# Silu ahead of quantising, two hidden rows by turns, and GpSimd's two norms in the other order

## The chip, the cores and the metric

The kernel runs on one NeuronCore of one Trainium2 chip. The time is device microseconds (us) of that core, the median of three runs. Five engines work side by side, each through its own list of instructions in order, and wait for each other by semaphores: TensorE (PE in the profile: matmuls and transposes; PEld is its weight load), VectorE (DVE), ScalarE (ACT), GpSimd (POOL), and SyncE (SP), which here only starts DMAs. TensorE's clock has two levels, 2.4 and 1.2 GHz; a granted clock of 1.00 in the profile is the upper one, 0.50 the lower.

## The reference

The input x has 4 x 1024 rows of 256 values. Three layers follow each other, each on a layer norm of x and each added to x. What matters here is the second half:

```python
x = x + attn(layernorm(x))                      # gated linear recurrence along the sequence
out = softmax(q k^T) v @ Wout                   # cross attention, 16 heads, 64 + 1 null keys
x = x + (out - mu) * rsqrt(var + 1e-6) * ln_scale + ln_bias
z = act_quant(layernorm(x))                     # round(z * 127 / max|z|), row by row
h = silu(z @ w_gate.T) * (z @ w_up.T)           # 1024 hidden values per row
x = x + act_quant(h) @ w_down.T                 # again scaled by 127 / max|h| of its row
```

The weights of the last layer are ternary (-1, 0, 1 times one scale), so its matmuls run on small integers in bf16 and the scales are put on behind them.

## The kernel before

The 4096 rows are 32 tiles of 128 rows (T = 32), a tile's rows on the 128 partitions. Stage 1 (the recurrence) takes four tiles at a time, then weights are folded, and from about 163 us on `stages2_3(n, u4)` runs for n = -2 to 38, on each engine with its own body. This is a software pipeline written out by hand: one step n works on several tiles at once, each one stage further on. The order of the calls in each body is the order in which that engine works; nothing is reordered.

What step n does, with the lines of the profile:

- PE: scores of tile n+2 (L1140), transposes of the attention weights of tile n in two halves (L1360, L1368) and of the null column (L1372), gate and up matmuls of tile n-5 (`gate_up`, L1140 with wgT and wuT), the output matmuls of tile n (L1382, L1387, and L1390, which ends them and signals `out_psum`). In even steps four more transposes follow for the scores of tiles n+4 and n+5 (L1273). Last is the down matmul of tile n-7 (L1140 with wdT). The first half of the scores of a later tile shares PSUM banks with gate, the second half with up, so gate waits until VectorE has read the first half of tile n+2's scores, and up until it has read the second.
- DVE: maximum and subtraction of tile n+2's scores, each in two halves (L991, L994, twice), the small part of the null column (L1057), in odd steps L965, the sum of exponentials of tile n+1 (L1003) and its reciprocal (L1008, `rden`), the statistics for the fourth norm of tile n-2 (L1072, L1080, `mv4`), silu times up of tile n-5 (`hidden_layer`, L1021), the maximum of z of tile n-3 (L1086), the statistics of the attention output of tile n (L1093, L1099, `mv3`), the maximum of the hidden row (L1028), scales (L1108 to L1032) and the last residual of tile n-7 (L1039).
- ACT: the attention output's norm of tile n-1 (`norm_out`, L686), copies of the transposed weights (L742, L745, L747), quantising the hidden row of tile n-6 (L759), silu of the gate of tile n-5 (`silu_gate`, L698, ahead of it a table load L693), the fourth norm of tile n-3 (`norm3`, L706), in even steps L663 and L678, and the exponential of tile n+2 (L773 with its own table load).
- POOL: scale, bias and residual of the attention output of tile n-1 (L516, L518, L520), attention weights times `rden` of tile n+1 (L528, L531), the cast of tile n-6's quantised row to bf16 (L540), then two groups of three tiny instructions that turn a mean and a variance into scale and bias: for the fourth norm of tile n-2 (L548, L550, L554, `sc4`) and for the attention output's norm of tile n (L561, L563, L567, `sc3`). Last is the rounding of z of tile n-3 (L574, L579).
- SP: DMA transposes of the quantised rows, z (L460) and hidden (L454), and the stores (L463).

The hidden layer has one row buffer `sg3` for silu's result and one, `h`, for the product; `hidden(n)` names the latter (for the last five tiles it goes by turns with the space of the exponentials). So silu of a tile waits until VectorE has read `sg3` for the tile before, and VectorE's product waits until ScalarE has quantised the row before. `late(n)` is true from n = 32 on; there ScalarE does silu ahead of quantising already.

Of the kernel before, what the change touches and what calls it, by code (L numbers as in the profile page):

```python
# [23 lines left out]
ALU = mybir.AluOpType  # L24
ACT = mybir.ActivationFunctionType
AX = mybir.AxisListType
# [7 lines left out]
def decoder_layer(nc, x, ctx_in, w_qkva, gamma, Wq, Wkv, null_kv, Wout, ln_scale, ln_bias,  # L34
# [6 lines left out]
    FI = w_gate.shape[0]  # L41
    T = B * N // P
# [17 lines left out]
    with ExitStack() as stack:  # L60
# [11 lines left out]
        def banks(b, n):  # L72
            return psum[:, b:b + n, :]
# [15 lines left out]
        expo = sbuf("expo", [P, 2 * GT])  # L89
# [27 lines left out]
        mv3 = sbuf("mv3", [P, 2, 2])  # L117
        sc3 = sbuf("sc3", [P, 2, 3])
# [4 lines left out]
        amax = sbuf("amax", [P, 2, 2])  # L123
        qs = sbuf("qs", [P, 2, 2])
        qr = sbuf("qr", [P, 2, 2])
        zw = sbuf("zw", [P, 4, 2])
# [23 lines left out]
        def carve(region, spec):  # L150
            views, at = {}, 0
            for name, n in spec:
# [11 lines left out]
        c = carve(region_c, [("sg", FI), ("h", FI), ("n", 2 * D // 2),  # L164
                             ("nvsel", HC * NP), ("nq", FI // 2), ("nhT", FI // 2)])
        nvsel = c["nvsel"]
        sg3 = c["sg"]
        n3 = c["n"].bitcast(BF16).rearrange("p (r d) -> p r d", r=2)

        f = carve(region_b, [("wq", KD * INNER), ("wout", HC * D), ("ctx", 2 * CTX),  # L170
# [37 lines left out]
        z3 = s["z"].rearrange("p (r d) -> p r d", r=2)  # L208
        nT3 = s["nT"].bitcast(BF16).rearrange("p (r k n) -> p r k n", r=2, k=KD)
        nh3 = s["nh"].bitcast(BF16)  # L210
        h3 = [c["h"], s["e"][:, 0:FI]]
        nhT3 = [r["nhT"].bitcast(BF16).rearrange("p (k n) -> p k n", k=FC) for r in (s, c)]
        nq3 = c["nq"].bitcast(I16)

# [3 lines left out]
        consts_set = sem("consts_set")  # L218
# [74 lines left out]
        p_ready = sem("p_ready")  # L293
# [46 lines left out]
        def positive(value):  # L340

            return not isinstance(value, int) or value > 0

        def registers(eng, *values):

            return [value if isinstance(value, int) else eng.to_reg(value) for value in values]
# [12 lines left out]
        def exists(n, count):  # L361

            return not isinstance(n, int) or 0 <= n < count
# [9 lines left out]
        def late(n):  # L373

            return isinstance(n, int) and n >= T

        def hidden(n):

            return h3[1 if isinstance(n, int) and n >= T - 5 and (n - (T - 5)) % 2 == 0 else 0]

        def half(n):
            return n >> 1

# [86 lines left out]
        def _(pool):  # L470
# [40 lines left out]
            def stages2_3(n, u4):  # L511
# [23 lines left out]
                if exists(n - 6, T):  # L535

                    pool.wait_ge(hq_done, n - 5)
                    if positive(n - 6):
                        pool.wait_ge(nhT_ready[v], 16 * ((n - 7) // 2 + 1))
                    pool.tensor_copy(nh3, nq3).then_inc(nh_ready, 1)  # L540
                if exists(n - 2, T):

                    count, free = registers(pool, n - 1, n - 3)
                    pool.wait_ge(consts_set, 2)
                    pool.wait_ge(mv4_done, count)
                    if positive(free):
                        pool.wait_ge(z_ready, free)
                    pool.tensor_scalar(sc4[:, u, 0:1], mv4[:, u, 1:2], 1e-5, None, ALU.add).then_inc(ve4_done, 1)  # L548
                    pool.wait_ge(ve4_done, n - 1)
                    pool.tensor_tensor(sc4[:, u, 1:2], sc4[:, u, 0:1], expo[:, 0:1], ALU.pow).then_inc(rstd4_done, 1)  # L550
                    count, = registers(pool, n - 1)
                    pool.wait_ge(consts_set, 2)
                    pool.wait_ge(rstd4_done, count)
                    pool.tensor_scalar(sc4[:, u, 2:3], mv4[:, u, 0:1], sc4[:, u, 1:2], -1.0, ALU.mult, ALU.mult) \  # L554
                        .then_inc(nmr4_done, 1)
                if exists(n, T):

                    count, = registers(pool, n + 1)
                    pool.wait_ge(consts_set, 2)
                    pool.wait_ge(mv3_done, count)  # L560
                    pool.tensor_scalar(sc3[:, u, 0:1], mv3[:, u, 1:2], 1e-6, None, ALU.add).then_inc(ve3_done, 1)  # L561
                    pool.wait_ge(ve3_done, n + 1)
                    pool.tensor_tensor(sc3[:, u, 1:2], sc3[:, u, 0:1], expo[:, 0:1], ALU.pow).then_inc(rstd3_done, 1)  # L563
                    count, = registers(pool, n + 1)
                    pool.wait_ge(consts_set, 2)
                    pool.wait_ge(rstd3_done, count)
                    pool.tensor_scalar(sc3[:, u, 2:3], mv3[:, u, 0:1], sc3[:, u, 1:2], -1.0, ALU.mult, ALU.mult) \  # L567
                        .then_inc(nmr3_done, 1)
                if exists(n - 3, T):

                    count, = registers(pool, n - 2)
# [14 lines left out]
        def _(act):  # L586
# [103 lines left out]
            def silu_gate(n, v):  # L690

                if n < T - 1:
                    act.preload_act_table(ACT.Silu)  # L693
                act.wait_ge(gate_psum, n - 4)
                act.wait_ge(zw_done, n - 4)
                if positive(n - 5):
                    act.wait_ge(h_ready, n - 5)
                act.activation(sg3, banks(0, 2).rearrange("p b n -> p (b n)"), ACT.Silu,  # L698
                               scale=zw[:, (n - 5) % 4, 0:1]).then_inc(silu_ready, 1)

            def norm3(n, v):
# [28 lines left out]
            def stages2_3(n, u4):  # L730
# [6 lines left out]
                if exists(n, T):  # L737

                    act.wait_ge(pT0_psum, n + 1)
                    if positive(n):  # L740
# [5 lines left out]
                    act.wait_ge(pT1_psum, n + 1)  # L746
                    act.activation(pT[:, HC // 2:HC, :], bank(5).rearrange("p (c n) -> p c n", n=P), ACT.Copy) \  # L747
                        .then_inc(pT1_ready, 1)
                if late(n) and exists(n - 5, T):
                    silu_gate(n, v)  # L750
                if exists(n - 6, T):

                    if n - 1 < T:
                        act.wait_ge(qr_done, n - 3)
                    else:
                        act.wait_ge(qrh_done, n - T)
                    if positive(n - 6):
                        act.wait_ge(nh_ready, n - 6)
                    act.activation(nq3, hidden(n - 6), ACT.Copy, scale=qr[:, u, 0:1]).then_inc(hq_done, 1)  # L759
                if not late(n) and exists(n - 5, T):  # L760
                    silu_gate(n, v)
                if not late(n) and exists(n - 3, T):
                    norm3(n, v)
                if even:
# [14 lines left out]
        def _(dve):  # L779
# [231 lines left out]
            def hidden_layer(n, v):  # L1011

                dve.wait_ge(up_psum, n - 4)
                dve.wait_ge(zw_done, n - 4)
                dve.wait_ge(silu_ready, n - 4)
                if late(n):
                    dve.wait_ge(hq_done, n - 6)
                    dve.wait_ge(p_ready, 2 * T)
                elif positive(n - 5):
                    dve.wait_ge(hq_done, n - 5)  # L1020
                dve.scalar_tensor_tensor(out=hidden(n - 5), in0=banks(2, 2).rearrange("p b n -> p (b n)"),  # L1021
                                         scalar=zw[:, (n - 5) % 4, 1:2], in1=sg3, op0=ALU.mult, op1=ALU.mult) \
                    .then_inc(h_ready, 1)

            def hidden_max(n, v):

                dve.wait_ge(h_ready, n - 4)
                dve.tensor_reduce(amax[:, v, 0:1], hidden(n - 5), AX.X, ALU.max, apply_absolute_value=True) \  # L1028
                    .then_inc(hmax_done, 1)

            def hidden_weight(n, v):
# [397 lines left out]
```

## Time and profile before

| what | value |
|---|---|
| median of 3 runs (lowest, highest) | 540.6 us (540.0, 541.85) |
| time of the profiled execution | 540.44 us |
| its span, first to last instruction | 538.7 us |
| mean granted TensorE clock | 0.983 |
| busy PE, DVE, ACT, POOL | 481.4, 423.9, 324.0, 304.4 us |
| HBM traffic | 36 GB/s over the span |

The span has four stretches: up to about 90 us loads and the first layer, then the first layer and the folding of weights, from about 229 us the full pipeline of all stages in steps of some 10.7 us, and from about 477 us the end, where no scores are left. A timeline row gives start, length, engine, line, operation and in brackets for how long the engine sat idle before it and what ended that; without brackets there was no idle time worth naming. A busy share is an average over such stretches: TensorE is busy for 89% of the span, but its matmul ends are modelled, so a short wait is better read from the starts of its rows.

### The profile page before, as it was taken

What the parts mean: (1) busy time and instruction counts of PE and PEld (TensorE: products, weight loads), DVE (VectorE), ACT (ScalarE), POOL (GpSimd) and SP (SyncE); (2) the same over time, 40 slices, a digit from 0 to 9 for tenths busy, and PEclk for the clock granted to TensorE, in tenths of its full rate; (3) what the DMA queues carried; (4) which work ended last, traced back from release to release, by engine and by line L of the source; (5) the groups of instructions that cost most, each with busy time, mean ns of one, the idle gap of its engine ahead of it and who ended that gap; (6) DMA issues with size and microseconds to landing.
All of it is one profiled execution on the core that took longest, in us unless ns stands there. A gap on an engine that the chain in (4) does not pass through costs nothing.

```text
span 538.7 us, 9271 instructions
## 1 busy us (share of the span) xinstructions
PE 481.4 (89%) x2926; PEld 389.4 (72%) x2954; DVE 423.9 (79%) x936; ACT 324.0 (60%) x450; POOL 304.4 (57%) x482
## 2 busy tenths in 40 slices
PE   1889999989988989999999999999999999988662
PEld 0666787767767878788887887888878778866321
DVE  4899998968337676988888888888888888875673
ACT  4422233245333353797788888877878888685451
POOL 2211223710001668778778787887787878787631
PEclk9999999999999999999999999999999999998895
DMA  8995000240000000012321222121213211212242
GB/s 263 321 337 213 1 0 1 40 78 1 2 0 1 1 2 5 12 24 50 42 49 35 44 48 49 35 50 41 49 35 46 48 46 36 54 40 63 51 97 68
DMA packets 68173, 32.06 MB, mean 60 GB/s; under 512 B 50720, under 2 KB 66336, under 8 KB 68128
## 3 DMA queue, kind: packets, MB, share of 16 engines
q1 hardware_dynamic: 68128, 31.50, 23.3%
q8 instruction: 23, 0.38, 0.3%
q14 instruction: 22, 0.18, 0.1%
HBM read 15.24 MB, written 4.19 MB: 36 GB/s over the span
## 4 chain that ended last, share of the span: by engine, by line
POOL 31%; issue 23%; PE 21%; DVE 17%; DMA 4%; ACT 2%; POOLq 1%; DVEq 1%; SPq 0%; ACTq 0%
PE psum L1140 9%; POOL region_d L540 5%; POOL region_d L518 3%; POOL xs L520 3%; POOL region_d L516 3%; PE psum L1156 3%; POOL sc L563 3%; POOL sc L550 3%; DVE region_a L877 3%; PE psum L1382 2%; POOL region_d L574 2%; PE psum L1387 2%; POOL region_d L531 2%; POOL region_c L579 2%; DMA region_d<-region_d 2%
## 5 line engine op out<-in xcount | busy, mean ns | idle before, releaser
L528 POOL TENSOR_TENSOR region_d<-region_d,rden 128x1024 f32<-128x1024 f32 x32 | 60.9, 1902 | 100.7 <-DVE rden L1008 100.7
L1140 PE MATMUL psum<-Mhi,xT2hi 128*128 128x260 f32 x256 | 75.0, 293 | 0.2
L1140 PE MATMUL psum<-Mlo,xT2hi 128*128 128x260 f32 x256 | 72.4, 283 | 0.0
L1140 PE MATMUL psum<-Mhi,xT2lo 128*128 128x260 f32 x256 | 72.3, 282 | 0.0
L1382 PE MATMUL psum<-VW,region_d 128*128 128x256 f32 x256 | 62.6, 389 | 4.6 <-DVE pTn L1057 4.6
L1387 PE MATMUL psum<-VW,region_d 128*128 128x256 f32 x256 | 60.7, 380 | 0.0
L1021 DVE SCALAR_TENSOR_TENSOR region_c<-psum,zw,region_c 128x1024 f32<-128x1024 f32 x29 | 37.2, 1283 | 28.7 <-ACT region_c L698 28.7
L1382 PEld LDWEIGHTS psum<-VW,region_d 128*128 128x128 f32 x256 | 49.0, 193 | 14.9 <-DVE pTn L1057 6.0
L1387 PEld LDWEIGHTS psum<-VW,region_d 128*128 128x128 f32 x256 | 49.0, 191 | 6.8
L686 ACT ACTIVATE region_d<-psum,sc 128x256 f32<-128x256 f32 x32 | 18.0, 564 | 55.7 <-POOL sc L567 54.8
L991 DVE TENSOR_REDUCE mx<-psum 128x8 f32<-128x520 f32 x64 | 44.2, 691 | 6.4 <-PE psum L1140 5.2
L1140 PEld LDWEIGHTS psum<-Mhi,xT2hi 128*128 128x128 f32 x256 | 48.2, 188 | 1.3 <-issue 1.0
L1140 PEld LDWEIGHTS psum<-Mlo,xT2hi 128*128 128x128 f32 x256 | 48.3, 189 | 0.0
L1140 PEld LDWEIGHTS psum<-Mhi,xT2lo 128*128 128x128 f32 x256 | 48.2, 188 | 0.0
L994 DVE TENSOR_TENSOR region_d<-psum,mx 128x520 f32<-128x520 f32 x64 | 44.8, 700 | 2.2
L494 POOL TENSOR_TENSOR pw_out<-pw_in,expo 128x8 f32<-128x8 f32 x8 | 13.1, 1641 | 52.6 <-DVE pw_in L811 52.6
L540 POOL CAST region_d<-region_c 128x1024 bf16<-128x1024 int16 x32 | 33.2, 1037 | 14.5 <-ACT region_c L759 14.5
L1003 DVE TENSOR_REDUCE den<-region_d 128x16 f32<-128x1040 f32 x32 | 39.4, 1231 | 0.5
L1140 PE MATMUL psum<-wuT,region_d 128*128 128x512 bf16 x128 | 33.9, 388 | 5.8 <-DVE region_d L994 3.2
L698 ACT ACTIVATE region_c<-psum,zw 128x1024 f32<-128x1024 f32 x32 | 35.6, 1112 | 5.2 <-DVE region_c L1021 2.9
L773 ACT ACTIVATE region_d<-region_d 128x1040 f32<-128x1040 f32 x32 | 34.3, 1073 | 7.2 <-DVE region_d L994 6.9
L598 ACT ACTIVATE region_a<-psum 128x1024 f32<-128x1024 f32 x8 | 8.2, 1028 | 47.3 <-PE psum L1156 47.3
(143 smaller groups left out, 1242.2 us busy)
## 6 DMA issues: line engine op xcount, KB each, us to landing
out_dram<-xs SPq DMA_DIRECT2D x32, 128.0 KB, 1.9
xs<-in_x_dram SPq DMA_DIRECT2D x1, 2560.0 KB, 13.9
VW<-in_L_xattn_Wkv_dram SPq DMA_DIRECT2D x1, 2048.0 KB, 11.9
region_b<-in_L_xattn_Wkv_dram SPq DMA_DIRECT2D x1, 2048.0 KB, 17.6
xs<-in_x_dram SPq DMA_DIRECT2D x3, 512.0 KB, 7.0
region_w<-in_L_ffn_w_gate_dram SPq DMA_DIRECT2D x2, 512.0 KB, 10.3
region_w<-in_L_ffn_w_up_dram SPq DMA_DIRECT2D x2, 512.0 KB, 7.9
region_w<-in_L_ffn_w_down_dram SPq DMA_DIRECT2D x8, 128.0 KB, 4.5
```

What stands on the lines that cost most here:

```text
L528: pool.tensor_tensor(p2[:, v, 0:H * MK].rearrange("p (h j) -> p h j", j=MK), e[:, :, 0:MK], rden[:, v, :].unsqueeze(2).broadcast_to([P, H, ...
L540: pool.tensor_copy(nh3, nq3).then_inc(nh_ready, 1)
L686: act.activation(y2[:, v, :], bank(7, D), ACT.Identity, bias=sc3[:, v, 2:3], scale=sc3[:, v, 1:2]).then_inc(y2_ready, 1)
L698: act.activation(sg3, banks(0, 2).rearrange("p b n -> p (b n)"), ACT.Silu, scale=zw[:, (n - 5) % 4, 0:1]).then_inc(silu_ready, 1)
L773: act.activation(e2[:, u, :], e2[:, u, :], ACT.Exp).then_inc(exp_done, 1)
L991: dve.tensor_reduce(mx[:, hh, :].rearrange("p (b h) -> p b h", h=HB), scores, AX.X, ALU.max) \
L994: dve.tensor_tensor(e2[:, u, hh * 2 * HB * J:(hh + 1) * 2 * HB * J].rearrange("p (b h j) -> p b h j", b=2, j=J), scores, mx[:, hh, :].rear ...
L1003: dve.tensor_reduce(den[:, :], e2[:, slot, :].rearrange("p (h j) -> p h j", j=J), AX.X, ALU.add) \
L1021: dve.scalar_tensor_tensor(out=hidden(n - 5), in0=banks(2, 2).rearrange("p b n -> p (b n)"), scalar=zw[:, (n - 5) % 4, 1:2], in1=sg3, op0= ...
L1140: mm = pe.matmul(dst, lhsT, rhs, start=i == 0, stop=i == len(terms) - 1)
L1382: pe.matmul(bank(7, D), pT[:, pair, :], VW[:, batch(n), pair, :], start=pair == 0, stop=False)
L1387: pe.matmul(bank(7, D), pT[:, pair, :], VW[:, batch(n), pair, :], start=False, stop=False)
```

## The change

ScalarE now does silu of tile n-5 first and quantises the hidden row of tile n-6 after it, in all steps. For this two row buffers are used by turns, `hid3[0]` and `hid3[1]` (the former `sg` and `h`), one for each parity of the tile: silu writes its row into one, VectorE multiplies in place in the same one, and the next step quantises from it. `hidden()` and its use of the exponentials' space are gone. Silu now waits for `hq_done` of the tile two before instead of `h_ready` of the tile before, the product has no wait for `hq_done` any more, and quantising names `h_ready`. On GpSimd the group for the output's norm (`sc3`) now stands ahead of the one for the fourth norm (`sc4`).

```diff
-        sg3 = c["sg"]
+        hid3 = [c["sg"], c["h"]]
...
+                if exists(n, T):
+
+                    count, = registers(pool, n + 1)
+                    pool.wait_ge(consts_set, 2)
+                    pool.wait_ge(mv3_done, count)
+                    pool.tensor_scalar(sc3[:, u, 0:1], mv3[:, u, 1:2], 1e-6, None, ALU.add).then_inc(ve3_done, 1)
...
                 if exists(n - 2, T):
 
                     count, free = registers(pool, n - 1, n - 3)
...
-                if exists(n, T):
-
-                    count, = registers(pool, n + 1)
-                    pool.wait_ge(consts_set, 2)
-                    pool.wait_ge(mv3_done, count)
...
-                if positive(n - 5):
-                    act.wait_ge(h_ready, n - 5)
-                act.activation(sg3, banks(0, 2).rearrange("p b n -> p (b n)"), ACT.Silu,
+                if positive(n - 6):
+                    act.wait_ge(hq_done, n - 6)
+                act.activation(hid3[v], banks(0, 2).rearrange("p b n -> p (b n)"), ACT.Silu,
...
-                if late(n) and exists(n - 5, T):
+                if exists(n - 5, T):
                     silu_gate(n, v)
...
-                    act.activation(nq3, hidden(n - 6), ACT.Copy, scale=qr[:, u, 0:1]).then_inc(hq_done, 1)
-                if not late(n) and exists(n - 5, T):
-                    silu_gate(n, v)
+                    act.wait_ge(h_ready, n - 5)
+                    act.activation(nq3, hid3[u], ACT.Copy, scale=qr[:, u, 0:1]).then_inc(hq_done, 1)
...
-                if late(n):
-                    dve.wait_ge(hq_done, n - 6)
-                    dve.wait_ge(p_ready, 2 * T)
-                elif positive(n - 5):
-                    dve.wait_ge(hq_done, n - 5)
-                dve.scalar_tensor_tensor(out=hidden(n - 5), in0=banks(2, 2).rearrange("p b n -> p (b n)"),
-                                         scalar=zw[:, (n - 5) % 4, 1:2], in1=sg3, op0=ALU.mult, op1=ALU.mult) \
+                dve.scalar_tensor_tensor(out=hid3[v], in0=banks(2, 2).rearrange("p b n -> p (b n)"),
+                                         scalar=zw[:, (n - 5) % 4, 1:2], in1=hid3[v], op0=ALU.mult, op1=ALU.mult) \
```

ScalarE, a full step of the pipeline, before (region_c holds the hidden rows, psum ahead of L698 is the gate):

```order
L747 ACTIVATE region_d<-psum 128x512
L759 ACTIVATE region_c<-region_c,qr 128x1024
L693 ACT_TABLE_LOAD
L698 ACTIVATE region_c<-psum,zw 128x1024
L706 ACTIVATE region_d<-xs,sc4 128x256
```

and after:

```order
L742 ACTIVATE region_d<-psum 128x512
L688 ACT_TABLE_LOAD
L693 ACTIVATE region_c<-psum,zw 128x1024
L755 ACTIVATE region_c<-region_c,qr 128x1024
L701 ACTIVATE region_d<-xs,sc4 128x256
```

The table load and silu (L698, now L693) have moved ahead of quantising (L759, now L755); the norm behind them keeps its place.

GpSimd, a full step of the pipeline, before:

```order
L540 CAST region_d<-region_c 128x1024
L548 TENSOR_SCALAR sc4<-mv4 128x1
L550 TENSOR_TENSOR sc4<-sc4,expo 128x1
L554 TENSOR_SCALAR sc4<-mv4,sc4 128x1
L561 TENSOR_SCALAR sc3<-mv3 128x1
L563 TENSOR_TENSOR sc3<-sc3,expo 128x1
L567 TENSOR_SCALAR sc3<-mv3,sc3 128x1
L574 TENSOR_SCALAR region_d<-region_d,qr 128x256
```

and after:

```order
L535 CAST region_d<-region_c 128x1024
L541 TENSOR_SCALAR sc3<-mv3 128x1
L543 TENSOR_TENSOR sc3<-sc3,expo 128x1
L547 TENSOR_SCALAR sc3<-mv3,sc3 128x1
L556 TENSOR_SCALAR sc4<-mv4 128x1
L558 TENSOR_TENSOR sc4<-sc4,expo 128x1
L562 TENSOR_SCALAR sc4<-mv4,sc4 128x1
L569 TENSOR_SCALAR region_d<-region_d,qr 128x256
```

The three instructions of `sc3`, with their wait for the statistics of the output just computed, now stand ahead of the three of `sc4`, and ahead of everything that followed those.

## Rows read from the trace of the kernel before

**Rows 1.** The page's groups: count and busy, mean ns, idle before, releaser.

```profile
L1021 DVE SCALAR_TENSOR_TENSOR region_c<-psum,zw,region_c 128x1024 f32<-128x1024 f32 x29 | 37.2, 1283 | 28.7 <-ACT region_c L698 28.7
```

**Rows 2.** Timeline of DVE: start us, us, then the instruction, idle before it.

```profile
348.80 1.28 DVE L1021 SCALAR_TENSOR_TENSOR region_c<-psum,zw,region_c 128x1024 f32<-128x1024 f32 x1 [1.16 <-ACT region_c L698]
350.00 0.41 DVE L1086 TENSOR_REDUCE amax<-region_d 128x1 f32<-128x256 f32 x1
350.32 0.42 DVE L1093 BATCH_NORM_STATS2 st<-psum 128x6 f32<-128x256 f32 x1
350.85 0.18 DVE L1099 BATCH_NORM_AGGREGATE mv<-st 128x2 f32<-128x6 f32 x1
...
355.22 0.70 DVE L994 TENSOR_TENSOR region_d<-psum,mx 128x520 f32<-128x520 f32 x1
...
360.69 0.43 DVE L1093 BATCH_NORM_STATS2 st<-psum 128x6 f32<-128x256 f32 x1
...
487.11 1.28 DVE L1021 SCALAR_TENSOR_TENSOR region_c<-psum,zw,region_c 128x1024 f32<-128x1024 f32 x1 [1.95 <-ACT region_c L698]
```

**Rows 3.** Timeline of ACT around the same step.

```profile
345.03 1.14 ACT L759 ACTIVATE region_c<-region_c,qr 128x1024 int16<-128x1024 f32 x1
...
347.48 1.11 ACT L698 ACTIVATE region_c<-psum,zw 128x1024 f32<-128x1024 f32 x1
348.49 0.59 ACT L706 ACTIVATE region_d<-xs,sc 128x256 f32<-128x256 f32 x1
...
353.66 0.56 ACT L686 ACTIVATE region_d<-psum,sc 128x256 f32<-128x256 f32 x1 [2.19 <-POOL sc L567]
```

**Rows 4.** Timeline of PE: L1390 ends a tile's output matmuls, wuT is up.

```profile
349.17 0.47 PE L1390 MATMUL psum<-VWnull,pTn 80*128 80x256 f32 x1
...
355.98 1.04 PE L1140 MATMUL psum<-wuT,region_d 128*128 128x512 bf16 x4 [0.27 <-DVE region_d L994]
...
360.12 0.47 PE L1390 MATMUL psum<-VWnull,pTn 80*128 80x256 f32 x1
...
366.45 1.03 PE L1140 MATMUL psum<-wuT,region_d 128*128 128x512 bf16 x4
```

**Rows 5.** Timeline of PE, the step from tile 28 to tile 29.

```profile
467.32 0.47 PE L1390 MATMUL psum<-VWnull,pTn 80*128 80x256 f32 x1
...
473.56 1.04 PE L1140 MATMUL psum<-wuT,region_d 128*128 128x512 bf16 x4
```

**Rows 6.** Windows: stretch, its us, busy of PE, PEld, DVE, ACT, POOL, clock.

```profile
336.70:358.20 21.50, 20.86 (x136) 17.57 (x137) 18.59 (x39) 17.81 (x24) 16.75 (x29) 1.00 0.20 43
```

**Rows 7.** Timeline of POOL around the same step.

```profile
347.59 1.90 POOL L528 TENSOR_TENSOR region_d<-region_d,rden 128x1024 f32<-128x1024 f32 x1 [1.68 <-DVE rden L1008]
...
349.79 1.03 POOL L540 CAST region_d<-region_c 128x1024 bf16<-128x1024 int16 x1
...
358.07 1.90 POOL L528 TENSOR_TENSOR region_d<-region_d,rden 128x1024 f32<-128x1024 f32 x1 [1.20 <-DVE rden L1008]
```

**Rows 8.** Timeline of PE, tile 3, before the full pipeline.

```profile
207.89 0.31 PE L1372 MATMUL psum<-ident,region_d 128*80 128x128 f32 x1 [0.49 <-ACT region_d L686]
```

**Rows 9.** Timeline of PE, the last two tiles' attention (30 and 31).

```profile
481.60 0.63 PE L1368 MATMUL psum<-ident,region_d 128*128 128x128 f32 x4 [0.37 <-DVE xs L1039]
...
483.33 1.99 PE L1382 MATMUL psum<-VW,region_d 128*128 128x256 f32 x8 [0.68 <-DVE pTn L1057]
...
491.71 0.63 PE L1368 MATMUL psum<-ident,region_d 128*128 128x128 f32 x4 [1.48 <-DVE xs L1039]
...
493.13 3.52 PE L1382 MATMUL psum<-VW,region_d 128*128 128x256 f32 x8 [0.68 <-DVE pTn L1057]
```

**Rows 10.** Windows over those matmuls: columns as in Rows 6.

```profile
493.00:495.00 2.00, 1.87 (x5) 1.58 (x6) 0.68 (x3) 2.00 (x3) 1.92 (x3) 0.61 0.35 98
```

**Rows 11.** Timeline of POOL behind the last tile's output.

```profile
499.64 0.22 POOL L561 TENSOR_SCALAR sc<-mv 128x1 f32<-128x1 f32 x1 [2.81 <-DVE mv L1099]
...
501.25 0.48 POOL L574 TENSOR_SCALAR region_d<-region_d,qr 128x256 f32<-128x256 f32 x1 [0.30 <-DVE qr L1111]
```

More of the change, by code:

```diff
@@ L210, in decoder_layer @@
         nh3 = s["nh"].bitcast(BF16)
-        h3 = [c["h"], s["e"][:, 0:FI]]
         nhT3 = [r["nhT"].bitcast(BF16).rearrange("p (k n) -> p k n", k=FC) for r in (s, c)]
@@ L375, in late @@
             return isinstance(n, int) and n >= T
-        def hidden(n):
-            return h3[1 if isinstance(n, int) and n >= T - 5 and (n - (T - 5)) % 2 == 0 else 0]
         def half(n):
@@ L540, in stages2_3 @@
                     pool.tensor_copy(nh3, nq3).then_inc(nh_ready, 1)
+                if exists(n, T):
[3 more added lines that the diff above has]
+                    pool.tensor_scalar(sc3[:, u, 0:1], mv3[:, u, 1:2], 1e-6, None, ALU.add).then_inc(ve3_done, 1)
+                    pool.wait_ge(ve3_done, n + 1)
+                    pool.tensor_tensor(sc3[:, u, 1:2], sc3[:, u, 0:1], expo[:, 0:1], ALU.pow).then_inc(rstd3_done, 1)
+                    count, = registers(pool, n + 1)
+                    pool.wait_ge(consts_set, 2)
+                    pool.wait_ge(rstd3_done, count)
+                    pool.tensor_scalar(sc3[:, u, 2:3], mv3[:, u, 0:1], sc3[:, u, 1:2], -1.0, ALU.mult, ALU.mult) \
+                        .then_inc(nmr3_done, 1)
                 if exists(n - 2, T):
@@ L555, in stages2_3 @@
                         .then_inc(nmr4_done, 1)
-                if exists(n, T):
-                    count, = registers(pool, n + 1)
-                    pool.wait_ge(consts_set, 2)
-                    pool.wait_ge(mv3_done, count)
[L561 to L568, printed above, removed]
                 if exists(n - 3, T):
@@ L1027, in hidden_max @@
                 dve.wait_ge(h_ready, n - 4)
-                dve.tensor_reduce(amax[:, v, 0:1], hidden(n - 5), AX.X, ALU.max, apply_absolute_value=True) \
+                dve.tensor_reduce(amax[:, v, 0:1], hid3[v], AX.X, ALU.max, apply_absolute_value=True) \
                     .then_inc(hmax_done, 1)
```

## The prediction

> **What bounds the kernel now.** I began with the page's groups and looked for an engine that waits often in the full pipeline. VectorE's product of silu and up stands out: it waited 28.7 us in all for ScalarE's silu, in 26 of its instructions, 1.1 us a tile [rows 1]. That says who waits, not whether the end waits with it. So I laid the timelines of one pair of steps beside each other: steps 17 and 18, from 345 to 361 us.
>
> ScalarE first quantises (L759, from 345.03, 1.14 us), then loads a table, then does silu (L698, 347.48 to 348.59) [rows 3]. VectorE was free at 347.64, stood still 1.16 us and began at 348.80, 0.21 behind silu's end [rows 2]. Everything behind it came late: the output's statistics (L1093) began at 350.32, though the output matmuls had ended at 349.17 + 0.47 = 349.64 [rows 2, 4]. In step 18 L1093 began at 360.69, 0.10 behind the end of L1390 at 360.12 + 0.47 = 360.59 [rows 2, 4]. So in odd steps VectorE is 350.32 - 349.74 = 0.58 us late at this place, and in even steps it is not late at all, since there TensorE is what it waits for.
>
> Does TensorE wait for that? From L1093 VectorE works without a pause to the end of the second score half (L994, 355.22 + 0.70 = 355.92): 5.60 us [rows 2]. TensorE's up matmul needs that half and began at 355.98, 0.06 later, having waited [rows 4]. From the even L1390 at 360.12 to the next up at 366.45 it took 6.33 us with four transposes more in it, and no wait is named: TensorE's own work [rows 4]. The odd passage took 355.98 - 349.17 = 6.81 us [rows 4]. So the pipeline's period is a loop of two steps, TensorE's own work except in one passage, from the odd L1390 to the even up, where it runs through VectorE and, before that, through silu.
>
> **The change part by part.**
>
> **Silu ahead of quantising.** The table load and silu move ahead by the 1.14 us of L759 [rows 3]. Silu then ends at 348.59 - 1.14 = 347.45, the product can start 0.21 later, at 347.66, where VectorE becomes free (347.64): the wait of 1.16 is gone. The fourth norm (L706) keeps its place, since quantising and silu only swap: 348.49 to 349.08 [rows 3]. The maximum of z (L1086) needs it and could start at about 349.1 instead of 350.00, and L1093 0.32 behind it [rows 2], at about 349.45. By then the output matmuls haven't ended (349.64), so L1093 starts at 349.74, ruled by TensorE. That caps the gain of an odd step at 0.58, not 1.16. The new odd passage is 0.47 + 0.10 + 5.60 + 0.06 = 6.23 us against 6.81: 0.58 less. The trace has this case already: between tiles 28 and 29, a passage without the four transposes and with VectorE on time, it took 473.56 - 467.32 = 6.24 us [rows 5]. I take 6.81 - 6.24 = 0.57. The even passage with its 6.33 stays TensorE's. Eleven odd passages lie between steps 7 and 28: 11 x 0.57 = 6.3 us. A bound from above: in 21.50 us of two steps TensorE was busy 20.86 [rows 6], so no more than 0.64 a pair can be had, 7.0 in all. From below the bound is nothing, if another wait takes silu's place (a rival).
>
> What could that wait be? Quantising now ends 1.1 us later, at silu's old end of 348.6. GpSimd's cast (L540) asks for it at 349.79 [rows 7]: covered by 1.2 us. If that cover were gone, the cast and the norms behind it would be late by what is missing. Silu's new wait, `hq_done` of the tile two before, was fulfilled a step ago. VectorE's product loses its wait on quantising, and writing in place costs it nothing that I can see: same shapes, one operand from PSUM, one from the row buffer; 1.28 us as before.
>
> **Output's norm ahead of the fourth norm.** The three instructions of `sc3` come 1.3 us earlier (L561 to L574 without a wait would be 1.61 - 0.30 = 1.31 [rows 11]). `norm_out` (L686) had waited 2.19 us for them in step 18 and began at 353.66 [rows 3]. Now it is done before TensorE asks for its bank. What is late next there is the score half of VectorE, so in the full pipeline I cost this at nothing. Its wait, `mv3`, is a risk: behind it on GpSimd stand `sc4`, the rounding of z, the output's scale and bias, the residual and the next attention weights. L1099 ends at 350.85 + 0.18 = 351.03, GpSimd finishes the cast at 349.79 + 1.03 = 350.82 [rows 2, 7]; with L1093 0.58 earlier, `mv3` is there in odd steps, and in even ones it comes within 0.2 us of the cast. GpSimd has 1.20 us idle a step ahead of L528 [rows 7], which takes that in. `sc4` comes 1.3 us later; L706 wants it some 5 us on. Nothing.
>
> Outside the full pipeline it shows. In step 3 TensorE's L1372 waited 0.49 for `norm_out` [rows 8]: gain 0.5; the steps around it wait for TensorE. Behind the last tile it costs: L561 had waited for `mv3` until 499.64, with `sc4` long done, and the rounding of z (L574) began at 501.25 [rows 11]. Now two groups of 1.31 stand behind that wait: L574 at 499.64 + 2.62 = 502.3, 1.05 later, and the DMA transposes and gate matmuls of the end hang on it. Cost 1.05.
>
> **The last two tiles.** In step 30 the product waited 1.95 for silu [rows 2], and tile 31's second transposes waited 1.48 for VectorE's last residual [rows 9], which is some 2.5 us of VectorE's work behind that product. Silu comes 1.14 earlier by the swap and a few tenths more because `norm_out` is no longer late. I take 1.4 of the 1.48. Ends: 1.1 and 1.5.
>
> **The clock.** Tile 31's first output matmuls took 3.52 us where tile 30's took 1.99 [rows 9]: the granted clock was 0.61 in the mean of 493 to 495, so most of it at the lower level, 1.2 GHz [rows 10]. Ahead of this TensorE had idled 1.48 and 0.68 us; ahead of tile 30's, 0.37 and 0.68, and there it kept 2.4 GHz [rows 9]. TensorE arrives at tile 31 0.6 us earlier itself, since tile 30's transposes no longer wait for `norm_out`, and the residual 1.4 earlier: so it idles about 1.48 + 0.6 - 1.4 = 0.7 and 0.68. That is nearer to the case that kept the clock. I take 3.52 - 1.99 = 1.5 us as gained; the other end is nothing.
>
> **Sum.** 540.44 - 6.3 - 0.5 + 1.05 - 1.4 - 1.5 = 531.8 us of a profiled run; the median stands 0.16 above it: 531.9.
>
> **A rule that speaks against it.** Silu's product will now start together with GpSimd's long L528 (347.59 to 349.49) [rows 7] and run beside it in full. Before, it began at 348.80, in the midst of an L528, wasn't held, and took 1.28, its mean over all 29 [rows 1, 2]. The Trainium skill, "SBUF — State Buffer", section "SBUF: two separate sides", says that VectorE and GpSimd share one port pair under an exclusive lock, which a VectorE instruction with two SBUF inputs contends for, the later one blocking until the other ends. The product reads one row from PSUM and one from SBUF, and the trace shows no block; if its scale column counted as a second input, the rival below would hold.
>
> **The rivals.**
> - *The clock falls as before.* TensorE's wait for the residual shrinks less than I think. 1.5 us less: 533.4. What the trace has are two cases, and mine lies between them. Chance 0.22.
> - *A new wait takes half.* The fourth norm (L706) has only 0.3 us to spare ahead of L1093 (349.45 against 349.74). If copies on ScalarE run 0.3 us later in odd steps, then z and not the output rules L1093. That leaves about 0.28 a pair, 3.1 us: 535.1, or 536.6 with the lower clock. Against it: ScalarE's copies start when TensorE's transposes allow, and these are TensorE's own work. Chance 0.14.
> - *Nothing.* The up matmul is held by something else that came at the same time. Then only the ends count, 540.6 - 0.5 + 1.05 - 1.4 = 539.7, up to 541.1 without the gain at tile 31. Against it stands the 6.24 of [rows 5]. Chance 0.08.
> - *Slower: GpSimd's wait for `mv3` becomes the loop.* GpSimd's own round is 358.07 - 347.59 - 1.20 = 9.28 us [rows 7] in a step of 10.7 (21.4 a pair, [rows 4]: 4.14 + 6.33 + 4.14 + 6.81). It decides from `mv3` 1.4 us behind the end of the cast. With 1.7 the round is 11.0: 0.3 us on each of 23 steps, 547.5. The rows have `mv3` 0.2 behind it. Chance 0.08.
> - *Slower: the lock.* The product waits for L528's end at 349.49 instead of 347.66, ends at 350.8, and L1093 starts at about 351.1, 0.8 later than before; the even steps' too. 22 x 0.8 = 17.6: 558. The product at 348.80 speaks against it. Chance 0.02.
> - *More.* All of TensorE's 0.64 a pair, 0.7 more: 531.2, and a few tenths more at the end. Chance 0.06.
>
> **How the numbers follow.** My forecast, 531.9 with its own range of 531.3 to 532.8, has 0.40. The range from 530.4 to 536.8 takes in both bounds of the steady gain, the fallen clock and the half gain: 0.82. It leaves out no gain (0.08) and the slower cases (0.10). About 0.3%, 1.6 us, is what a measurement of this kernel can tell from no change. Faster by more: 0.40 + 0.22 + 0.14 + 0.06 = 0.82; within it 0.08; slower 0.10.
>
> **What the profile after would show.** Right: the product's idle before it nearly gone from the groups; L1093 instead waiting for L1390 in nearly all steps, some tenths in odd ones and up to 1 us in even ones; the odd passage from L1390 to up at 6.23 to 6.25 and the even one still 6.33; `norm_out` without its wait of 2 us; GpSimd waiting 0 to 0.2 us for `mv3`, and still for `rden`; the rounding of z behind the last tile 2.6 us after the first `sc3` instruction; the granted clock at 1.00 over tile 31's output matmuls. Wrong: an odd passage near 6.8 with an idle L1086 (z rules), a product of more than 1.3 us or held while L528 runs (lock), an L528 without idle time ahead (GpSimd rules), or a clock of 0.5 again at tile 31.

## The result

The changed kernel takes 535.05 us (median of 5 runs, 534.85 to 536.53), the kernel before 540.6: ratio 0.9908, 95% interval 0.9884 to 0.9931. In a second comparison, beside one of the experiments' kernels, it came to 534.93 against 541.94, ratio 0.9886 (0.9861 to 0.9910). So it is faster by about 1%. The forecast was 531.9, 8.7 us less than before; 5.6 us came. The result lies inside the stated range (530.4 to 536.8) and outside the forecast's own (531.3 to 532.8).

The page after, spans first, then the groups that answer to [rows 1]: VectorE's product is now L1010, silu L693, GpSimd's attention weights L523.

```profile
span 533.3 us, 9241 instructions
...
L523 POOL TENSOR_TENSOR region_d<-region_d,rden 128x1024 f32<-128x1024 f32 x32 | 60.9, 1904 | 93.3 <-DVE rden L1002 93.3
...
L1010 DVE SCALAR_TENSOR_TENSOR region_c<-psum,zw,region_c 128x1024 f32<-128x1024 f32 x32 | 41.0, 1282 | 4.2 <-ACT region_c L693 3.3
```

The product's idle time fell from 28.7 us over 29 tiles to 4.2 us over all 32, as meant. Its length didn't change (1282 ns against 1283), although in steps 17 and 18 it runs beside L523 from start to end (346.27 to 347.55 beside 346.15 to 348.06 in step 17).

The timeline of TensorE over steps 17 and 18, answering to [rows 4] (L1379 ends a tile's output matmuls, wuT is up, L1262 are the four transposes for the scores of later tiles):

```profile
347.74 0.47 PE L1379 MATMUL psum<-VWnull,pTn 80*128 80x256 f32 x1
...
353.98 1.04 PE L1129 MATMUL psum<-wuT,region_d 128*128 128x512 bf16 x4
...
358.12 0.47 PE L1379 MATMUL psum<-VWnull,pTn 80*128 80x256 f32 x1
358.76 0.66 PE L1262 MATMUL psum<-ident,region_d 128*128 128x128 f32 x4 [0.16 <-ACT region_d L658]
...
364.86 1.03 PE L1129 MATMUL psum<-wuT,region_d 128*128 128x512 bf16 x4
```

The odd passage, from L1379 to up, is 353.98 - 347.74 = 6.24 us: 0.57 less, to the hundredth what was forecast. But the even passage is 364.86 - 358.12 = 6.74 us, where it had been 6.33. The four transposes wait for ScalarE's L658, the second norm of tiles n+4 and n+5 (norm2 in what follows; L663 before). So 0.41 of the 0.57 is given back in these two steps. The same stretch on ScalarE and VectorE (answering to [rows 3] and [rows 2]):

```profile
352.46 0.60 ACT L737 ACTIVATE region_d<-psum 128x512 f32<-128x512 f32 x1 [1.05 <-PE psum L1349]
...
356.09 1.14 ACT L755 ACTIVATE region_c<-region_c,qr 128x1024 int16<-128x1024 f32 x1
357.13 0.59 ACT L701 ACTIVATE region_d<-xs,sc 128x256 f32<-128x256 f32 x1
357.62 1.08 ACT L658 ACTIVATE region_d<-xs,nmr,rstd 128x256 f32<-128x256 f32 x2
359.45 0.60 ACT L673 ACTIVATE xT2hi<-psum 128x512 fp32r<-128x512 f32 x1 [0.75 <-PE psum L1262]
```

```profile
357.75 0.42 DVE L1075 TENSOR_REDUCE amax<-region_d 128x1 f32<-128x256 f32 x1
358.70 0.43 DVE L1082 BATCH_NORM_STATS2 st<-psum 128x6 f32<-128x256 f32 x1 [0.53 <-PE psum L1379]
```

ScalarE works from L737, which starts when TensorE's transposes allow, to the end of norm2 at 357.62 + 1.08 = 358.70, without a pause; 0.06 later the four transposes begin. VectorE waits 0.53 us for TensorE in this step: it is no longer what holds it.

The same place in the kernel before (L1360 are a tile's first four transposes, L742 the copy of their result, L663 norm2, L1273 the four later transposes):

```profile
353.25 0.60 PE L1360 MATMUL psum<-ident,region_d 128*128 128x128 f32 x4
...
360.42 0.60 PE L1273 MATMUL psum<-ident,region_d 128*128 128x128 f32 x4
```

```profile
354.12 0.59 ACT L742 ACTIVATE region_d<-psum 128x512 f32<-128x512 f32 x1
...
359.23 1.08 ACT L663 ACTIVATE region_d<-xs,nmr,rstd 128x256 f32<-128x256 f32 x2
```

There norm2 ended at 359.23 + 1.08 = 360.31 and the four transposes began 0.11 later. TensorE's way from a tile's first transposes to the start of its last output matmul fell from 360.12 - 353.25 = 6.87 us to 358.12 - 351.83 = 6.29. ScalarE's chain from the first copy to norm2's end did not get shorter (6.19 and 6.24 us); it only starts sooner behind those transposes, 0.63 us against 0.87, because `norm_out` is no longer ahead of it.

**Where the 5.4 us between the two profiled spans went**, by the starts of L1390 and L1379 of all tiles. Up to step 7: 0.36 less. The eleven odd passages of steps 7 to 27: 74.7 to 69.4 us, 5.3 less. The eleven even ones of steps 8 to 28: 70.2 to 73.0, 2.7 more. Tiles 30 and 31: 3.1 less. Behind tile 31's output: 0.7 more. Below, "odd" and "even passages" are those of steps 9 to 27: the first two (7 and 8) and that of step 28, which has no four transposes (6.24 us before and after), differ.

### The profile page after: what moved, and what is told of

The parts are those of the page before. It is cut to its first block, busy times and chain, and to the rows that moved or that the text cites. A ratio compares the mean times of both kernels' runs of the same rounds, so it can differ in the third digit from the quotient of the medians.

```text
span 533.3 us, 9241 instructions
## 1 busy us (share of the span) xinstructions
PE 480.0 (90%) x2926; PEld 389.3 (73%) x2954; DVE 429.2 (80%) x936; ACT 325.4 (61%) x450; POOL 305.3 (57%) x482
## 4 chain that ended last, share of the span: by engine, by line
PE 54%; DVE 22%; issue 9%; ACT 7%; POOL 4%; DMA 4%; DVEq 1%; POOLq 0%; ACTq 0%
PE psum L1129 26%; PE psum L1371 8%; PE psum L1376 7%; PE psum L1145 3%; DVE region_d L988 3%; DVE region_a L871 3%; DVE mx L985 3%; ACT region_c L755 2%; DMA region_d<-region_d 2%; DVE amax L1017 2%; PE psum L1349 2%; PE psum L1232 2%; PE psum L1262 2%; ACT region_d L658 1%; PE psum L1249 1%
## 5 line engine op out<-in xcount | busy, mean ns | idle before, releaser
L523 POOL TENSOR_TENSOR region_d<-region_d,rden 128x1024 f32<-128x1024 f32 x32 | 60.9, 1904 | 93.3 <-DVE rden L1002 93.3
L1371 PE MATMUL psum<-VW,region_d 128*128 128x256 f32 x256 | 61.1, 381 | 4.8 <-DVE pTn L1046 4.8
L1376 PE MATMUL psum<-VW,region_d 128*128 128x256 f32 x256 | 60.5, 379 | 0.0
L1371 PEld LDWEIGHTS psum<-VW,region_d 128*128 128x128 f32 x256 | 48.1, 190 | 14.9 <-DVE pTn L1046 6.4
L1376 PEld LDWEIGHTS psum<-VW,region_d 128*128 128x128 f32 x256 | 48.6, 190 | 6.6
L1010 DVE SCALAR_TENSOR_TENSOR region_c<-psum,zw,region_c 128x1024 f32<-128x1024 f32 x32 | 41.0, 1282 | 4.2 <-ACT region_c L693 3.3
L755 ACT ACTIVATE region_c<-region_c,qr 128x1024 int16<-128x1024 f32 x32 | 36.4, 1139 | 5.5 <-DVE qr L1116 5.5
L1017 DVE TENSOR_REDUCE amax<-region_c 128x1 f32<-128x1024 f32 x32 | 38.2, 1193 | 0.4 <-issue 0.2
L693 ACT ACTIVATE region_c<-psum,zw 128x1024 f32<-128x1024 f32 x32 | 35.6, 1113 | 3.6 <-PE psum L1129 3.3
```

What stands on the lines that cost most here:

```text
L523: pool.tensor_tensor(p2[:, v, 0:H * MK].rearrange("p (h j) -> p h j", j=MK), e[:, :, 0:MK], rden[:, v, :].unsqueeze(2).broadcast_to([P, H, ...
L693: act.activation(hid3[v], banks(0, 2).rearrange("p b n -> p (b n)"), ACT.Silu, scale=zw[:, (n - 5) % 4, 0:1]).then_inc(silu_ready, 1)
L755: act.activation(nq3, hid3[u], ACT.Copy, scale=qr[:, u, 0:1]).then_inc(hq_done, 1)
L1010: dve.scalar_tensor_tensor(out=hid3[v], in0=banks(2, 2).rearrange("p b n -> p (b n)"), scalar=zw[:, (n - 5) % 4, 1:2], in1=hid3[v], op0=AL ...
L1017: dve.tensor_reduce(amax[:, v, 0:1], hid3[v], AX.X, ALU.max, apply_absolute_value=True) \
L1371: pe.matmul(bank(7, D), pT[:, pair, :], VW[:, batch(n), pair, :], start=pair == 0, stop=False)
```

## The experiments

The kernel before was measured again beside each set of kernels, and the ratios are to it: 539.95 us beside the first four, 540.0 beside the next four, 541.94 beside the last two, each set on a chip of its own.

**GpSimd's order undone.** The changed kernel with the two norm groups as before.

```diff
-                if exists(n, T):
-
-                    count, = registers(pool, n + 1)
-                    pool.wait_ge(consts_set, 2)
-                    pool.wait_ge(mv3_done, count)
...
                 if exists(n - 2, T):
...
+                if exists(n, T):
+
+                    count, = registers(pool, n + 1)
+                    pool.wait_ge(consts_set, 2)
+                    pool.wait_ge(mv3_done, count)
...
```

> GpSimd's two norm groups are back in the order of before; silu stays ahead of quantising. Theory: in the changed kernel the four transposes after an even tile's output wait for ScalarE's second norm (norm2), which stands at the end of ScalarE's chain transposed-weight copy, silu, quantise, fourth norm, norm2. With GpSimd's old order the output's norm comes about 6.0 us after the attention weights start, at 352.2 instead of 350.8 in the frame of the changed kernel's step 18, so norm_out ends 0.2 us after TensorE is ready for the first copy, and the chain and the transposes come 0.2 us later: 11 x 0.2 = 2.3 us, plus 0.5 lost in step 3 and some 0.5 at tiles 30 and 31, minus 0.9 at the end where z is rounded earlier: about 537.4 us. The even passage from output to up is near 6.95 us, the odd one 6.24. Rival (GpSimd's order costs nothing in the full pipeline, as the prediction had it): even passage 6.74 as in the changed kernel, 535.1 us.

Measured: 537.44 us, ratio 0.9958 (0.9940 to 0.9976) to before. Odd passages 6.23 to 6.25 but for two of 6.58 and 6.64, even ones 6.90 to 6.93 but for the two behind those. TensorE and ScalarE in step 18 of this run:

```profile
353.42 0.60 PE L1349 MATMUL psum<-ident,region_d 128*128 128x128 f32 x4
...
359.71 0.47 PE L1379 MATMUL psum<-VWnull,pTn 80*128 80x256 f32 x1
360.52 0.66 PE L1262 MATMUL psum<-ident,region_d 128*128 128x128 f32 x4 [0.35 <-ACT region_d L658]
```

```profile
353.81 0.56 ACT L681 ACTIVATE region_d<-psum,sc 128x256 f32<-128x256 f32 x1 [2.18 <-POOL sc L562]
354.27 0.59 ACT L737 ACTIVATE region_d<-psum 128x512 f32<-128x512 f32 x1
```

`norm_out` (L681) waits for GpSimd and puts L737 to 0.85 us behind the transposes' start at 353.42; in the changed kernel, with GpSimd's new order, it is 352.46 - 351.83 (the start of L1349 there) = 0.63. The chain to norm2 is late by that, and the four transposes start 0.81 behind L1379 against 0.64. So GpSimd's order is worth 2.4 us once silu is ahead. Of this 1.8 lie in the full pipeline (about 0.17 in an even passage, 0.3 in step 8), where the prediction had nothing; between the ends of the two profiles, 0.6 up to step 7 and 1.1 at tiles 30 and 31 are gained and 1.15 behind tile 31's output lost.

**GpSimd's order alone.** The kernel before with only its two groups exchanged.

> The kernel before with GpSimd's output norm ahead of the fourth norm, silu still behind quantising. Theory: silu still holds the product, so the odd passage stays at 6.8 us and the even one at 6.3; gain 0.5 in step 3 and 0.3 at tile 30, cost about 1 us where z is rounded behind the last tile: 540.8 us, no change that can be measured. Rival (the earlier output norm also carries a share of the gain in the full pipeline, since ScalarE's chain in even steps started 0.28 us late for it): 11 x 0.28 = 3 us less, 537.8.

Measured: 539.57 us, ratio 0.9999 (0.9978 to 1.0020). Odd passages 6.80 to 6.81, even ones 6.35 to 6.37, as before. Without silu ahead it is worth nothing that can be measured: 0.5 us less in step 3, 0.3 in steps 7 and 8, 0.3 at tile 30, and behind the last tile 41.1 us (span's end 536.6, tile 31's L1390 at 495.5) against 40.5, 40.0 and 40.1 in three profiles of the kernel before. But it does give ScalarE's chain room: from norm2's end to the four transposes it is 0.3 us now in even steps from 10 on, where it was 0.06 to 0.12.

**norm2 in the odd steps, on the changed kernel.** The wait that the profile names is taken away by doing norm2 one step earlier, where ScalarE idles.

```diff
-                if even:
-                    act.wait_ge(xT2_psum, half(n) + 1)
-                    norm2(n + 4, 2 * (u4 // 2))
-                    norm2(n + 5, 2 * (u4 // 2) + 1)
+                if u == 1 and exists(n + 1, T - 4):
+                    act.wait_ge(xT2_psum, half(n + 1) + 1)
+                    norm2(n + 5, 2 * ((u4 + 1) % 4 // 2))
+                    norm2(n + 6, 2 * ((u4 + 1) % 4 // 2) + 1)
```

> The changed kernel, with ScalarE's two norm2 instructions taken out of the even step and put into the odd step before it, behind the fourth norm, where ScalarE idles 0.8 and 1.05 us in the two waits that follow. Theory (norm2 behind quantising holds the four transposes): the transposes wait for nothing, the even passage falls from 6.74 to 6.33, the odd one stays at 6.24: 11 x 0.41 = 4.5 us less, 530.5 us. Rival (the even passage is held by something else that is late at the same time, such as z or the product in even steps): the transposes no longer wait for norm2, but the up matmul or the output does, and the time stays within 1 us of 535.

Measured: 533.32 us (531.44 to 533.53), ratio 0.9861 (0.9832 to 0.9889). Even passages 6.34 to 6.36, odd ones 6.24 to 6.27 but for two of 6.56 and 6.60. In step 18:

```profile
358.15 0.47 PE L1379 MATMUL psum<-VWnull,pTn 80*128 80x256 f32 x1
358.45 0.60 PE L1262 MATMUL psum<-ident,region_d 128*128 128x128 f32 x4
```

The transposes wait for nothing and start 0.30 behind L1379. From tile 0's output to tile 31's it is 312.1 us against 315.3: 3.2 less. The forecast of 4.5 counted the gain in eleven passages; only eight of them had the full wait (8 x 0.39 = 3.1): three of the even ones follow a longer odd passage or have no transposes. What is left up to the profiled execution's 533.53 is a clock that fell at 170 to 175 us (below). The other five executions have no profile; three of them took 533.3 to 533.4 us at nearly the same mean clock (0.979 or 0.980), two 531.4 and 531.6 at 0.988 and 0.983. The theory holds; its size was 1.3 us too large.

**The same move on the kernel before.**

> The kernel before, with the same move of norm2. Theory: there norm2 ended at 360.31 and the transposes began at 360.42, 0.30 us behind the start of L1390, as late as in odd steps the down matmul began without any wait: norm2 came exactly in time, so moving it gives nothing: within 0.8 us of 540.6, odd passage 6.8, even one 6.3. Rival (norm2 already held TensorE in before, hidden in the 6.33): the even passage falls under 6.25 and the kernel gains 1 us or more.

Measured: 538.87 us, ratio 0.9981 (0.9962 to 1.0001). The median is 1.1 us under the 539.95 measured beside it, an interval that takes in no change. Odd passages 6.79 to 6.82 but for 6.70 in step 9, even ones 6.34 to 6.39, as before (6.80 to 6.82, and 6.33 to 6.41 in its three profiles). Besides step 9 only step 8 became shorter, 6.45 against 6.69 to 6.71: there norm2 had held the transposes already. Elsewhere it cost next to nothing; it is the change that gave it a price.

**How tight was norm2 before?** The kernel before with one more ScalarE instruction ahead of norm2 in even steps.

```diff
                 if even:
+                    act.wait_ge(ln_loaded, 32)
+                    act.activation(s["free"], ls_bc[:, :], ACT.Identity)
                     act.wait_ge(xT2_psum, half(n) + 1)
```

> The kernel before, with one more ScalarE instruction in even steps ahead of norm2, a 128x256 copy of a constant into unused space (about 0.49 us of ScalarE's time, by the start-to-start of the fourth norm, which has its shape). Theory: norm2 was exactly in time before the change, so each even passage with the four transposes grows by nearly the whole 0.49, from 6.36 to about 6.85, while the odd ones stay at 6.8: 10 x 0.49 = 4.9 us more, some 545. Rival (ScalarE had room in even steps, and the wait of the changed kernel comes from elsewhere): passages and time unchanged.

Measured: 543.91 us (541.29 to 544.17), ratio 1.0069 (1.0046 to 1.0092). Odd passages unchanged at 6.80 to 6.82, even ones 6.63 to 6.66. ScalarE in step 18 of this run, and TensorE (L1392 and L1275 are its L1390 and L1273):

```profile
360.70 0.41 ACT L766 ACTIVATE region_d<-ls_bc 128x256 f32<-128x256 f32 x1
361.01 1.08 ACT L663 ACTIVATE region_d<-xs,nmr,rstd 128x256 f32<-128x256 f32 x2
```

```profile
361.59 0.47 PE L1392 MATMUL psum<-VWnull,pTn 80*128 80x256 f32 x1
362.14 0.66 PE L1275 MATMUL psum<-ident,region_d 128*128 128x128 f32 x4
```

The added instruction took 0.31 us of ScalarE's time, not 0.49, and the transposes start 0.55 behind L1392, where the kernel before has 0.30 to 0.31 (step 18: 360.42 - 360.12). So of 0.31 us, about 0.24 came through: before the change norm2 had 0.07 us to spare in this step. Wherever the transposes wait for norm2 they start 0.05 us behind its end; in the kernel before they started 0.06 to 0.12 behind it from step 10 on, so it had 0.01 to 0.07. Between two profiled spans that both kept the clock at tile 31 it is 539.5 against 536.8, 2.7 us on ten passages. The medians differ by 3.9 us (4.9 was forecast); the five slower executions have no profile, and what the further 1.2 us are stays open.

**The last tile's order.** The kernel with norm2 moved, and at the last tile alone the fourth norm ahead of the output's norm again.

```diff
-                if exists(n, T):
+                if exists(n, T) and n < T - 1:
...
                     pool.wait_ge(mv3_done, count)
...
                 if exists(n - 2, T):
...
                     pool.wait_ge(mv4_done, count)
...
+                if n == T - 1:
+
+                    count, = registers(pool, n + 1)
+                    pool.wait_ge(consts_set, 2)
+                    pool.wait_ge(mv3_done, count)
...
```

> The changed kernel with norm2 in the odd steps (as in the run before), and at the last tile alone GpSimd's fourth norm stands ahead of the output's norm again. Theory: behind the last output GpSimd waits for its statistics with both groups behind it, which puts the rounding of z 1.05 us later; with the fourth norm done during that wait the stretch from the start of L1379 of tile 31 to the span's end falls from 41.2 us to about 40.1, and the whole to about 1 us under the kernel with norm2 moved (533.3): 532.3. Rival (the end hangs on another path, the DMA transposes of the hidden rows): the stretch stays at 41 us.

Measured: 530.79 us (530.70 to 530.83), ratio 0.9828 (0.9805 to 0.9851): the fastest of all. GpSimd behind the last output, in the run with norm2 moved, and then in this one:

```profile
492.00 0.23 POOL L541 TENSOR_SCALAR sc<-mv 128x1 f32<-128x1 f32 x1 [1.11 <-DVE mv L1088]
...
494.71 0.48 POOL L569 TENSOR_SCALAR region_d<-region_d,qr 128x256 f32<-128x256 f32 x1
```

```profile
490.77 0.22 POOL L569 TENSOR_SCALAR sc<-mv 128x1 f32<-128x1 f32 x1
...
492.06 0.48 POOL L582 TENSOR_SCALAR region_d<-region_d,qr 128x256 f32<-128x256 f32 x1
```

From the first `sc3` instruction to the rounding of z it takes 2.71 us with both groups in between and 1.29 with one. From the start of tile 31's last output matmul (490.54 and 488.91) to the span's end (531.7 and 529.0) it takes 41.2 and 40.1: 1.1 less, as expected. The other 1.6 us between the two profiles was there before the edit can act: it is the clock that fell ahead of tile 0's output in the one. The two ran on different chips. Behind the last output all four profiles with `sc3` first there took 41.1 to 41.2 us, and of the eight with `sc4` first six took 40.0 to 40.1 and two 40.5 and 41.0.

**Silu ahead and norm2 moved, GpSimd's order as before.**

> Silu ahead of quantising and norm2 in the odd steps, but GpSimd's groups in the order of before everywhere. Theory: GpSimd's new order mattered in the full pipeline (537.4 against 535.05) only because ScalarE's chain ended in norm2, for which TensorE waited; with norm2 gone from even steps it matters no more: passages 6.24 and 6.36, as with the new order, and the whole differs only at the ends: 0.5 slower in step 3, 1.1 at tiles 30 and 31, 1.05 faster behind the last tile, about 532 us (530.4 from the profile without a fallen clock plus 1.6 minus 1.05 = 531.3). Rival (the output's norm holds something else in even steps as well, its bank or the copies): even passages stay 0.15 or more above 6.36 and the kernel is at 533 or above.

Measured: 533.86 us (532.07 to 534.42), ratio 0.9865 (0.9835 to 0.9896). Even passages 6.34 to 6.36, odd ones 6.24 to 6.26 but for two: no trace of GpSimd's order left in the full pipeline, as the theory said. The three differences at the ends came too: step 3 0.5 longer, tiles 30 and 31 1.1 longer, the end 1.1 shorter. The median lies in the rival's range all the same; it is the profiled execution (532.07, span 530.3) that is near the 532 expected. The other three (533.8 to 534.4) were not profiled; their mean granted clock was 0.981 to 0.983 against 0.988, so the clock is a likely cause, but not shown.

**The kernel before, twice more.**

> The kernel before once more, for its profile: does TensorE's clock fall at tile 31 in each execution? Theory: it falls in some executions and not in others with the same idle times ahead of it, since two variants with the same idle times (1.47 to 1.49 and 0.68 us) kept it; then this one takes 9.8 or 11.5 us from tile 30's to tile 31's last output matmul and 538.3 to 540.4 in all. Rival (before always loses it): 11.5 us.

> The same kernel a second time, for the same question: 9.8 us if the clock is kept at tile 31 and 11.5 if it falls. Before falling in all three profiles would speak for the rival.

Measured: 538.59 and 540.24 us. Windows over tile 31's output matmuls, TensorE alone (stretch, its us, busy, granted clock, DMA share, GB/s), first of the one and then of the other:

```profile
490.00:492.00 2.00, 0.51 (x6) 1.00 0.61 116
492.00:494.00 2.00, 1.32 (x8) 1.00 0.15 32
494.00:496.00 2.00, 2.00 (x11) 1.00 0.21 67
```

```profile
490.00:492.00 2.00, 0.50 (x5) 1.00 0.53 98
492.00:494.00 2.00, 1.32 (x8) 0.90 0.15 33
494.00:496.00 2.00, 2.00 (x6) 0.50 0.24 71
```

TensorE had been idle for the same time in both. In the first the clock stayed at 2.4 GHz, in the second it fell to 1.2. (Idle times ahead of tile 31's second transposes and output matmuls: 1.50 and 0.68 us in both.) From tile 30's to tile 31's last output matmul they took 9.81 and 11.50 us.

**The changed kernel once more.**

> The changed kernel once more, beside the others on one chip, and for its passages. Theory: odd 6.24, even 6.74, within 1 us of 535.05. Rival (the 0.41 of the even passage was a matter of that one execution): even passage 6.4.

Measured: 534.93 us, odd passages 6.23 to 6.25, even ones 6.72 to 6.76 but for two (steps 10 and 24, each behind a long odd passage). The even passage's 0.4 us is no matter of one execution.

## Why the prediction was half right

By its own steps:

- *Silu ahead of quantising frees the product; the odd passage falls from 6.81 to 6.24; the output and not silu then rules L1093.* Right. The product starts as soon as VectorE is free in odd steps and waits 0.2 us for silu in even ones, L1082 waits for L1379 in nearly all steps, and the cap of 0.57 instead of 1.16 is what came. The eleven odd passages gave 5.3 us and not 6.3. Step 7 could give only 0.35, since it took 6.60 before. And two odd passages (9 and 23) stayed at 6.56 and 6.62, which took 0.7; they did so, within 0.03 us, in all six profiles with silu ahead. In both VectorE stops between the output's statistics and the scores: in step 9 by 0.3 us ahead of L1017 and in step 23 by 0.37 ahead of L1088, at the same place in every profile and with no other engine named. The kernel before has neither stop; why they come is open. In the changed kernel the even passages behind them are shorter by as much (6.43 and 6.37 against 6.74), so in sum they cost it nothing.
- *The even passage with its 6.33 stays TensorE's.* This is the step that failed. It had "no wait named", and the prediction took that for room. ScalarE's chain from the copies to norm2 ended at most 0.07 us before TensorE needed it, as the experiment with one more instruction shows. When the odd passage gave TensorE 0.57 us, ScalarE's chain followed by only part of it: swapping silu and quantising leaves the chain's length as it was, and what let it end sooner was only that `norm_out` no longer delayed L737. In step 18 the room adds up. Without GpSimd's order it was 0.07 us, so the transposes should start 0.57 - 0.07 = 0.50 us later behind the last output matmul, and they do (0.81 against 0.30). With it the room is 0.25 (0.30 - 0.05, from the run with GpSimd's order alone), which leaves 0.32, and it is 0.64 against 0.30. The even passage grew by 0.41 in all, 2.7 us over the eleven. The two norm2 runs show it: moved in the changed kernel, the passage is 6.35; moved in the kernel before, only steps 8 and 9 change.
- *GpSimd's order costs and brings nothing in the full pipeline.* Wrong for the same reason. It brings 0.17 us a pair while norm2 ends the chain (537.44 without it, 535.05 with it) and nothing otherwise (539.57 on the kernel before; the same passages with norm2 moved). Its gain in step 3 (0.5 forecast, 0.5 measured) and its cost behind the last tile (1.05 us forecast; 41.2 against 40.1 us to the span's end in the run on the last tile's order, 1.1) were right.
- *The wait for `mv3` is taken in by GpSimd's idle time.* Right: 14 waits in the full pipeline, mostly 0.3 us where 0 to 0.2 was expected, with 0.5 to 1.8 us of idle time ahead of L523 left in every step. (Of the page's 93.3 us ahead of L523, 56.1 are its first wait, ahead of the pipeline.)
- *Tiles 30 and 31, 1.4 us.* Right: against the profile of before that kept its clock it is 9.02 + 9.81 - 8.44 - 8.92 = 1.47. One reading was off: from the product's end (487.11 + 1.28) to the residual's end VectorE took 3.2 us, not some 2.5; the forecast didn't use it.
- *The clock, 1.5 us.* Over tile 31's output matmuls the clock stayed up in the changed kernel's profiles, as forecast. But that TensorE's idle time ahead of it would decide was read from two cases of one execution, and it doesn't decide alone. Of six profiles with 1.47 to 1.50 and 0.68 us of idle time, three of them of the kernel before, only two lost the clock, both of them of the kernel before. All six with silu ahead, where the first idle time is 0.61 us, kept it; whether that is more than chance six profiles don't show. So the 1.7 us gained here are in part luck: the profile that the forecast started from was one with a fallen clock.
- *The rivals.* "A new wait takes half" named 535.1, which is what came, but by the fourth norm and VectorE. VectorE's L1075 does start 1.42 us behind the product's start in step 17, where it was 1.20, but VectorE still waits 0.2 us for L1379 behind it, so that isn't it: that this rival's number fits is luck. The lock did not show: the product is as long as ever beside L523, so in this trace its scale column doesn't count as a second input from SBUF.

The sum with the measured terms, between the profiled spans: 538.7 - 0.4 (up to step 7) - 5.3 + 2.7 - 3.1 (tiles 30 and 31, 1.7 of it the clock) + 0.7 = 533.3. The profiled execution came 3.2 us above the forecast of 531.8: 2.7 by the even passages, which were put at nothing, and 1.0 by the odd ones, less 0.4 at the ends.

## What to carry to other kernels

A passage in which no wait is named isn't a passage with room: look at how long before its use each input was ready, on every engine, above all at the end of the longest chain (here norm2, at most 0.07 us). When a loop of several engines is shortened by x, each other chain that closes the loop must be able to follow by x; an exchange of two instructions inside such a chain doesn't shorten it. And an edit that is worth nothing by itself (GpSimd's order, norm2 in another step) can be worth 2.4 and 3.2 us beside one that moves the bound.

## What the runs showed of the hardware

I had not expected the clock to differ between executions of the same kernel. With the same instructions and the same idle times TensorE's granted clock fell at tile 31 in two of three profiled executions of the kernel before, for 1.7 us more. What decides it is open. In the run with norm2 moved it fell in another place, ahead of tile 0's output, and in the one with the last tile's order it didn't (windows of TensorE, first of the one, then of the other):

```profile
165.00:170.00 5.00, 3.98 (x31) 1.00 0.01 3
170.00:175.00 5.00, 3.83 (x20) 0.66 0.00 0
```

```profile
165.00:170.00 5.00, 3.68 (x29) 1.00 0.01 3
170.00:175.00 5.00, 4.13 (x29) 1.00 0.00 0
```

Tile 0's last output matmul started at 178.44 and 176.61 us. Steps of 1.6 to 1.9 us between executions of one kernel (538.6 and 540.2; 531.4 and 533.3) have the size of one such fall, though only some of these executions have a profile that shows it. Single profiles are therefore better compared from passage to passage than by their ends.
